# Attention value product by pairs of query tiles, with the context as the stationary operand

## Chip, cores and metric

One Trainium2 chip, of which the kernel uses one core. The metric is the device time of one execution in microseconds (us); the result of a kernel is the median of its runs.

## The reference

One decoder layer on x of 4 batches x 512 tokens x 256 features, float32, with three residual blocks:

```python
x = x + min_gru(layernorm(x))                 # forward and backward recurrence, then W_out
x = x + cross_attention(layernorm(x), ctx)    # the part that changes
x = x + product_key_ffn(layernorm(x))

# cross attention: ctx is (4, 1601, 256), one head
q = x @ Wq.T; k = ctx @ Wk.T; v = ctx @ Wv.T
out = softmax(q @ k.T / 16) @ v
```

The kernel folds the weights: M = Wq.T Wk is made once, the scores are (x M) ctx.T, and the values are (P ctx) Wv.T, so that only the context itself is an operand of the two large products. P is the matrix of exponentials, which is not normalised; its row sums divide the result.

## The kernel before

The kernel has three stages: `stage_gru`, `stage_attention` and `stage_ffn`. The first two share one block of code for each engine, so that they run into each other; the third begins when all engines are through the second.

Large products are done in split form: an operand is held as a high half (fp32r, copied by ScalarE) and a low half (original minus high, made by VectorE, or by GpSimd for the context), and a product is three matmuls, high x high, high x low, low x high (`split_products`, L75 to L77, and L984 to L986).

**Tiles and slots.** The 2048 tokens are 16 query tiles of 128 rows (`TILES`), four to a batch (`TPB`). The context of a batch has 1601 rows: 13 tiles of 128 (`CT`, the last one has 65 rows), in four groups (`GROUPS`: 4, 4, 4, 1). The work is a pipeline of slots g = 0 to 17. Slot g begins on TensorE with the scores of tile g: four blocks (`KB`) of up to 402 columns, six matmuls each, into the four banks of pS (`scores`, L950). The items of the slot follow, in the order that `ORDER` (L574) and `at_tile` write out; every engine goes through the same list and does its own part of each item, in order:

- E: exponentials of tile g on ScalarE, two instructions (L800, L803), once VectorE has the row maximum (`row_max`, L859, one reduction per score block).
- P0 to P3 of tile g-1: TensorE transposes the probabilities of one group into a bank of pR (L1018); ScalarE copies it as the high half (`high`, L754), VectorE makes the low half (`low`, L842).
- A0 to A3 of tile g-1: the value product of one group, 3 matmuls of 256 columns per context tile, into pA. The weights are the transposed probabilities, the moving operand is the context (L984 to L986).
- V of tile g-2: ScalarE has copied pA to `val`, multiplied by the inverse row sum (`values`, L761); TensorE transposes it (two transposes, L1023), ScalarE and VectorE make the halves.
- O of tile g-2: the product with Wv, six matmuls of 256 columns; VectorE adds it to x (`output`, L849). S: the moments of the new rows (`new_moments`, L854).
- X and Q: the transposes of the normalised rows of the next batch (two items of four transposes) and their product with M (two items of six matmuls of 512 columns). The rows are normalised by VectorE (`normalise`, L827) at the end of its slot. Slots 16 and 17 hold the X of the next stage.
- F: the first products of the next stage, in slot 17.

V0 and P0 are issued on TensorE ahead of the last score block (`EARLY`, L597), and their low halves on VectorE there too (`LOWS`).

**Banks and waits.** X, Q, P, V and O use the three banks of pR in turn (`RING` = 3, `place` is an item's number in the ring): TensorE takes a bank when the item three places earlier has been read by VectorE. The two transposed halves of P are one buffer each, pTh and pTl.

**Context.** While a batch is worked on, the context of the next comes in: 15 pieces (`PIECES`), eight of the transposed form for the scores and seven of the plain form for the values (six of 128x512, the last 65x256). A slot has four of them, the fourth slot of a batch three (`pieces_at`, L654). SyncE loads a piece into one of four raw buffers, ScalarE copies the high half (`piece_high`, L769), GpSimd makes the low half (L750). ScalarE takes a piece right after P0, P2 and P3 (`BESIDE`, L596, used in L810), and what is left at the end of its list. The scores of the first tile of a batch wait for all 15 pieces:

```python
            if b >= 1 and t == 0:
                pe.wait_ge(piece_lo, PIECES * b)
```

The weights of the next stage (wqh, wql, two pieces in slots 12 and 13, and `down`) have buffers of their own. `roots` and `new_roots` on GpSimd raise variances to the power -1/2.

Of the kernel before, what the change touches and what calls it, by code (L numbers as in the profile page):

```python
# [554 lines left out]
def stage_attention(nc, keep, d, ctx, sems):  # L555
# [18 lines left out]
    ORDER = "V P0 P1 E O P2 S A0 P3 A1 A2 A3"  # L574

    def at_tile(g):
        out = []
        for kind in ORDER.split():
            a = g - {"V": 2, "O": 2, "S": 2, "E": 0}.get(kind[0], 1)
# [3 lines left out]
        ahead = 1 if b == 1 else 0  # L583
        if b < BATCH and g % TPB == 1 - ahead:
            out += [("X", b, 0), ("X", b, 1)]
        if b < BATCH and g % TPB == 2 - ahead:
            out += [("Q", b, 0), ("Q", b, 1)]
        if g == TILES:
            out.insert(out.index(("P", TILES - 1, 3)), ("X", BATCH, 0))
            out.insert(out.index(("A", TILES - 1, 1)), ("X", BATCH, 1))  # L590
        if g == TILES + 1:
            v, o, s = out
            out = [("F", 0, 0), v, ("F", 0, 1), ("X", BATCH + 1, 0), o, ("X", BATCH + 1, 1), s, ("F", 0, 2), ("F", 0, 3)]
        return out

    BESIDE = ("P0", "P2", "P3")  # L596
    EARLY = {"V0": 3, "P0": 3}  # L597

    def between_scores(g, j):

        return [it for it in SLOTS[g] if g < TILES and EARLY.get(f"{it[0]}{it[2]}") == j]

    LOWS = {"V0": 3, "P0": 3}

    def lows(g, j):

        return [it for it in SLOTS[g] if g < TILES and LOWS.get(f"{it[0]}{it[2]}") == j]

# [3 lines left out]
    SLOTS = [at_tile(g) for g in range(TILES + 2)]  # L612
    ring = [it for slot in SLOTS for it in slot if it[0] not in "ESAF"]
# [8 lines left out]
    qT1 = [st.sb(n, [P, DC, SEQ], F32R) for n in ("qT1h", "qT1l")]  # L622
    qT = (qT0, qT1)
    pT = [st.sb(n, [P, CT, P], F32R) for n in ("pTh", "pTl")]
    vT = [st.sb(n, [P, 2, DC, P], F32R) for n in ("vTh", "vTl")]
    val = st.sb("val", [P, 2, D])
# [5 lines left out]
    rinv = st.sb("rinv", [P, 2])  # L632
    stats = st.sb("stats", [P, TILES, 6])
    ve, rstd, ve3 = (st.sb(n, [P, TILES]) for n in ("ve", "rstd", "ve3"))
    halves(st, keep, 1)
# [11 lines left out]
    value_mm, val_ready, x3_ready = st.sem("value_mm"), st.sem("val_ready"), st.sem("x3_ready")  # L647
# [20 lines left out]
    def wait_context(eng, i):  # L668
# [3 lines left out]
        b, n = i // PIECES + 1, i % PIECES  # L672
        if 2 <= b < BATCH:
            if n < DC * -(-CTX // SEQ):
                eng.wait_ge(score_mm, KB * TPB * (b - 1))
            else:
                eng.wait_ge(value_mm, NG * TPB * (b - 1))

    def half(it, which, n):
# [7 lines left out]
        if kind == "P":  # L687
            rows = CLAST if GROUPS[i][-1] == CT - 1 else P
            m = len(GROUPS[i])
            return pT[which][0:rows, GROUPS[i][0]:GROUPS[i][0] + m], \  # L690
                bank[0:rows, 0:m * P].rearrange("p (t n) -> p t n", n=P)
        return vT[which][:, a % 2], bank[:, 0:DC * P].rearrange("p (t n) -> p t n", n=P)

    def wait_overwrite(eng, it):
# [8 lines left out]
        elif kind == "P" and a >= 1:  # L703
            eng.wait_ge(value_mm, NG * (a - 1) + i + 1)
        elif kind == "V" and a >= 2:
            eng.wait_ge(bank_full, place[("O", a - 2, 0)] + 1)

    def sync(sp):
# [5 lines left out]
        sp.dma_start(bq[:], d["fbq"]).then_inc(ld_bq, 16)  # L714
        sp.dma_start(keep["down"][:], d["downT"].rearrange("(k p) n -> p k n", p=P)).then_inc(ld_key, 16)
# [9 lines left out]
    def gpsimd(pool):  # L725
# [15 lines left out]
        for g in range(TILES):  # L741
            if g == 2:
                roots(1, 2 * TPB, TILES)
            if g >= TPB and g % TPB == 2:
                new_roots(g // TPB - 1)
            for i in pieces_at(g):
# [3 lines left out]
                pool.tensor_tensor(lo, raw(i % RAW), hi.bitcast(F32), ALU.subtract).then_inc(piece_lo, 1)  # L750

    def scalar(act):
# [8 lines left out]
        def values(g):  # L761
            act.wait_ge(value_mm, NG * (g + 1))
            act.wait_ge(rinv_ready, g + 1)
            if g >= 2:
                act.wait_ge(bank_full, place[("V", g - 2, 0)] + 1)
            act.activation(val[:, g % 2], pA[:, 0:D], ACT.Copy, scale=rinv[:, g % 2:g % 2 + 1])\
                .then_inc(val_ready, 1)
# [21 lines left out]
        for g in range(TILES + 2):  # L789
            if 0 <= g - 2 < TILES:  # L790
                values(g - 2)
            left = list(pieces_at(g)) if g < TILES else []
            for it in SLOTS[g]:
# [14 lines left out]
                elif it[0] not in "SAO":  # L808
# [6 lines left out]
    def vector(dve):  # L815
# [43 lines left out]
        def row_max(g):  # L859

            h = g % 2
            for j in range(KB):
                for it in lows(g, j):
                    low(it)
# [4 lines left out]
            for it in lows(g, KB):  # L869
                low(it)  # L870
# [22 lines left out]
        for g in range(TILES + 2):  # L893
            if 0 <= g - 1 < TILES:
                h = (g - 1) % 2
                dve.wait_ge(exp_ready, 2 * g)
                if g >= 3:
                    dve.wait_ge(val_ready, g - 2)
                link(dve.tensor_tensor(rowsum[:, h:h + 1], part[:, h, 0:1], part[:, h, 1:2], ALU.add))
                dve.reciprocal(rinv[:, (g - 1) % 2:(g - 1) % 2 + 1], rowsum[:, (g - 1) % 2:(g - 1) % 2 + 1])\  # L900
# [7 lines left out]
            for it in SLOTS[g]:  # L908
                if it[0] == "O":
# [3 lines left out]
                elif it[0] not in "AEF" and it not in [i for j in range(KB + 1) for i in lows(g, j)]:  # L913
                    low(it)
# [5 lines left out]
            if TPB < g < TILES and g % TPB == 1:  # L920
                a = g - 1 - TPB
# [3 lines left out]
            if g >= TILES - 1 and g <= TILES:  # L925
                normalise(BATCH + g - TILES + 1)

    def tensor(pe):
# [42 lines left out]
        def item(it):  # L971
            kind, a, i = it
            if kind == "A":
                pe.wait_ge(bank_free, place[("P", a, i)] + 1)
                if i == 0 and a >= 1:
                    pe.wait_ge(val_ready, a)
                if i == 0 and a == 0:
                    pe.wait_ge(gru["x2_ready"], 2 * BATCH)
                    pe.wait_ge(gru["piece_lo"], PIECES)
                for kt in GROUPS[i]:  # L980
                    rows, par = (CLAST if kt == CT - 1 else P), (a // TPB) % 2
                    l = [p[0:rows, kt] for p in pT]
                    r = [c[par][0:rows, kt] for c in (cNh, cNl)]
                    pe.matmul(pA[:, 0:D], l[0], r[0], start=(kt == 0), stop=False)  # L984
                    pe.matmul(pA[:, 0:D], l[0], r[1], start=False, stop=False)  # L985
                    last = pe.matmul(pA[:, 0:D], l[1], r[0], start=False, stop=(kt == CT - 1))  # L986
# [33 lines left out]
            elif kind == "V":  # L1020
                pe.wait_ge(val_ready, a + 1)
                for k in range(DC):
                    last = pe.transpose(bank[:, k * P:(k + 1) * P], val[:, a % 2, k * P:(k + 1) * P], ident[:])  # L1023
            else:
                pe.wait_ge(bank_free, place[("V", a, 0)] + 1)
                last = split_products(pe, bank[:, 0:D], [
                    ((vT[0][:, a % 2, k], vT[1][:, a % 2, k]), (WvTh[:, k], WvTl[:, k])) for k in range(DC)])
            last.then_inc(bank_full, 1)

        for g in range(TILES + 2):  # L1030
# [5 lines left out]
            for it in SLOTS[g]:  # L1036
                if it[0] not in "ES" and it not in early(g):
# [5 lines left out]
def stage_ffn(nc, keep, d):  # L1043
# [28 lines left out]
    with ExitStack() as ctx:  # L1072
        st = Stage(nc, ctx, "ffn")
        down = keep["down"]
# [772 lines left out]
def program(nc, d):  # L1847
    with ExitStack() as ctx:
# [5 lines left out]
        for n in ("wqh", "wql"):  # L1854
            keep[n] = st.sb(n, [P, DC, QC * P], F32R)
# [78 lines left out]
```

## Time and profile before

| | us |
|---|---|
| median of 3 runs | 416.8 |
| lowest and highest | 416.44, 419.18 |
| the profiled execution, its own time | 418.28 |
| its span, first to last instruction | 416.4 |

The profile is of one execution. Its rows give, for an engine (PE is TensorE, PEld its weight loads, DVE VectorE, ACT ScalarE, POOL GpSimd), the start and duration of instructions, and what ended the idle time before them. Matmuls overlap: the time that one costs is the distance between two starts, not its duration. Instructions of one kind in a row are merged (x4), and the time is then that of all.

### The profile page before, as it was taken

Reading aid. Unit: us, or ns where it says so; the run is one execution under the profiler, and the core shown is the slowest. Engines: PE = TensorE matmul, PEld = TensorE weight load, DVE = VectorE, ACT = ScalarE, POOL = GpSimd, SP = SyncE. Lnnn points to the kernel's source line nnn. Section 1 sums busy time; section 2 is a strip of 40 time slices with the busy share of each in tenths; the row PEclk is TensorE's granted clock in tenths of the full one; section 3 lists DMA queues with packets and bytes.
Section 4 is the critical chain, followed back from the end, with each engine's and each line's share of the span. In section 5 each row is a group of like instructions: output and inputs, shape, how many; then the busy total and the mean of one; then the engine's idle time right before and its main releaser. Section 6 shows DMA issues by size and latency. Waiting matters only on the chain. (4 is left out here: it accounts for less than half of the span.)

```text
span 416.4 us, 7868 instructions
## 1 busy us (share of the span) xinstructions
PE 396.5 (95%) x2569; PEld 366.5 (88%) x2569; DVE 296.9 (71%) x1104; ACT 243.7 (59%) x535; POOL 215.9 (52%) x208
## 2 busy tenths in 40 slices
PE   1999999999999999999999999999999979999877
PEld 1788888899899999999999999999778979999766
DVE  4889677786466676457575555565785998899996
ACT  3687759354465655456574534444566878677362
POOL 2588999764253224334333212000147777889994
PEclk9999999999999999999999999999999987999999
DMA  7800223004422222221232100000100000000101
GB/s 229 291 0 3 76 56 100 9 5 126 108 67 64 55 80 76 60 78 53 58 96 58 54 2 2 0 2 0 28 1 2 0 3 1 27 26 28 41 25 65
DMA packets 19992, 21.38 MB, mean 51 GB/s; under 512 B 3180, under 2 KB 16624, under 8 KB 19952
## 3 DMA queue, kind: packets, MB, share of 16 engines
q1 hardware_dynamic: 18832, 19.96, 16.4%
q10 hardware_dynamic: 1120, 0.92, 0.7%
q8 instruction: 21, 0.34, 0.4%
q14 instruction: 19, 0.16, 0.1%
HBM read 18.78 MB, written 2.10 MB: 50 GB/s over the span
## 5 line engine op out<-in xcount | busy, mean ns | idle before, releaser
L847 DVE TENSOR_TENSOR att_pTl<-context_pR,att_pTh 128x512 fp32r<-128x512 f32 x64 | 37.4, 586 | 26.4 <-ACT att_pTh L759 26.2
L1191 POOL TENSOR_TENSOR ffn_prod<-ffn_first,ffn_near 128x1024 f32<-128x1024 f32 (+1 forms) x29 | 54.1, 1884 | 2.1 <-DVE ffn_first L1591 2.1
L866 DVE TENSOR_REDUCE att_mx<-keep_pQ 128x1 f32<-128x402 f32 x64 | 35.3, 567 | 24.2 <-PE keep_pQ L77 24.2
L759 ACT ACTIVATE att_pTh<-context_pR 128x512 fp32r<-128x512 f32 x64 | 32.4, 516 | 9.8 <-PE context_pR L1018 9.0
L1743 PE MATMUL ffn_pT<-keep_ident,ffn_prod 128*128 128x128 f32 x240 | 31.9, 291 | 6.2 <-POOL ffn_prod L1191 3.7
L1743 PEld LDWEIGHTS ffn_pT<-keep_ident,ffn_prod 128*128 128x128 f32 x240 | 30.0, 153 | 8.6 <-DVE ffn_hT L1622 4.8
L223 POOL TENSOR_TENSOR gru_z<-gru_z,gru_g 128x512 f32<-128x512 f32 x16 | 28.8, 1799 | 7.9 <-DVE gru_g L428 7.9
L1018 PE MATMUL context_pR<-keep_ident,att_prob 128*128 128x128 f32 (+1 forms) x208 | 32.8, 272 | 0.0
L984 PE MATMUL context_pA<-context_cNh,att_pTh 128*128 128x256 f32 (+1 forms) x104 | 31.4, 302 | 0.9 <-DVE att_pTl L847 0.9
L984 PE MATMUL context_pA<-att_cNh,att_pTh 128*128 128x256 f32 (+1 forms) x104 | 31.1, 299 | 0.0
L1553 DVE MAX8 ffn_top<-ffn_e 128x8 f32<-128x32 f32 x256 | 29.2, 177 | 0.4 <-ACT ffn_e L1359 0.2
L750 POOL TENSOR_TENSOR att_cNl<-keep_raw,att_cNh 128x512 fp32r<-128x512 f32 (+1 forms) x14 | 16.7, 1210 | 24.3 <-ACT att_cNh L773 24.3
L985 PE MATMUL context_pA<-context_cNl,att_pTh 128*128 128x256 f32 (+1 forms) x104 | 29.2, 281 | 0.0
L759 ACT ACTIVATE att_vTh<-context_pR 128x256 fp32r<-128x256 f32 x16 | 6.1, 384 | 39.4 <-PE context_pR L1023 39.4
L986 PE MATMUL context_pA<-context_cNh,att_pTl 128*128 128x256 f32 (+1 forms) x104 | 29.1, 280 | 0.0
L986 PE MATMUL context_pA<-att_cNh,att_pTl 128*128 128x256 f32 (+1 forms) x104 | 29.0, 279 | 0.0
L985 PE MATMUL context_pA<-att_cNl,att_pTh 128*128 128x256 f32 (+1 forms) x104 | 29.0, 279 | 0.0
L750 POOL TENSOR_TENSOR att_cTl<-keep_raw,att_cTh 128x512 fp32r<-128x512 f32 (+1 forms) x16 | 15.4, 978 | 25.9 <-ACT att_cTh L773 25.9
L75 PE MATMUL keep_pQ<-gru_xTh,gru_wh 128*128 128x512 f32 x62 | 26.9, 434 | 0.0
L1018 PEld LDWEIGHTS context_pR<-keep_ident,att_prob 128*128 128x128 f32 (+1 forms) x208 | 24.8, 140 | 0.7
L76 PE MATMUL keep_pQ<-gru_xTl,gru_wh 128*128 128x512 f32 x62 | 24.6, 397 | 0.0
L77 PE MATMUL keep_pQ<-gru_xTh,gru_wl 128*128 128x512 f32 x62 | 24.6, 396 | 0.0
(326 smaller groups left out, 1297.3 us busy)
## 6 DMA issues: line engine op xcount, KB each, us to landing
keep_raw<-in_ctxT SPq DMA_DIRECT2D x24, 256.0 KB, 2.6
keep_raw<-in_ctx SPq DMA_DIRECT2D x24, 256.0 KB, 2.8
out<-keep_x SPq DMA_DIRECT2D x16, 128.0 KB, 1.7
keep_x<-in_x SPq DMA_DIRECT2D x3, 512.0 KB, 9.9
gru_wout<-in_W_out SPq DMA_DIRECT2D x1, 512.0 KB, 8.0
keep_raw<-in_fWq SPq DMA_DIRECT2D x2, 256.0 KB
keep_raw<-in_ctxT SPq DMA_DIRECT2D x8, 32.5 KB, 4.1
keep_raw<-in_ctx SPq DMA_DIRECT2D x4, 65.0 KB
```

The costliest lines, as they stand in the source:

```text
L223: pool.tensor_tensor(z[:, n % ZB], z[:, n % ZB], g[:, u % 2], ALU.mult).then_inc(zg_ready, 1)
L750: pool.tensor_tensor(lo, raw(i % RAW), hi.bitcast(F32), ALU.subtract).then_inc(piece_lo, 1)
L759: act.activation(to, bank, ACT.Copy).then_inc(bank_high, 1)
L847: dve.tensor_tensor(to, bank, half(it, 0, n)[0].bitcast(F32), ALU.subtract).then_inc(bank_free, 1)
L866: last = dve.tensor_reduce(mx[:, h, j:j + 1], pS[:, j, 0:min(SPANS[j][1], CTX) - SPANS[j][0]], AX.X, ALU.max)
L984: pe.matmul(pA[:, 0:D], l[0], r[0], start=(kt == 0), stop=False)
L985: pe.matmul(pA[:, 0:D], l[0], r[1], start=False, stop=False)
L986: last = pe.matmul(pA[:, 0:D], l[1], r[0], start=False, stop=(kt == CT - 1))
L1018: last = pe.transpose(bank[0:rows, m * P:(m + 1) * P], prob[:, a % 2, kt * P:kt * P + rows], ident[:])
L1191: return eng.tensor_tensor(prod[:, i % PB, a:b].rearrange("p h (i j) -> p h i j", j=KEYS), (factor if factor is not None else first[:, n % ...
L1553: ins = dve.max(top[:, n % 2, t, h, a:a + 2 * TOPK], e[:, n % 2, t, h, half * KEYS:(half + 1) * KEYS])
L1743: last = pe.matmul(pW[:, i % 2, c * P:(c + 1) * P], prod[:, i % PB, h, c * P:(c + 1) * P], ident[:], start=(h == 0), stop=(c == 0 and h == ...
```

## The change

- Tiles go in pairs (even, odd). pTh and pTl are twice as wide, one half per tile. The value product (items A and B) has the context tile as weights, half of the features each (A the first, B the second), and the transposed probabilities of both tiles as the moving operand, 256 columns. Its result is the transposed value directly, in pA.
- There is no V transpose and no `val`. V is now one copy of pA (512 columns) on ScalarE and one low half on VectorE, per pair.
- The inverse row sum is no longer applied to the values: `output` multiplies by it as it adds to x.
- The order is written out for even and odd slots, with one slot more at the end (g = 18), and own lists for slots 1, 16, 17 and 18. In even slots both O are issued ahead of the third score block and P0, P1 ahead of the fourth.
- ScalarE takes pieces of the context only at the end of its list (`BESIDE` is gone). Which slot has which pieces, and the wait of the scores for them, stay.
- wqh, wql and `down` share the space of the first context buffers; the loads wait for the scores of the third batch. `new_roots` and the variances before it come two slots later.

```diff
-    ORDER = "V P0 P1 E O P2 S A0 P3 A1 A2 A3"
+    EVEN = "O-4 O-3 P0-1 P1-1 P2-1 E S-4 S-3 A0-2 P3-1 A1-2 A2-2 A3-2"
+    ODD = "B0-3 E P0-1 B1-3 P1-1 B2-3 P2-1 B3-3 V-3 P3-1"
...
+        if g == 0:
+            out += [("X", 1, 0), ("X", 1, 1)]
+        if g == 1:
+            out = [("E", 1, 0), ("P", 0, 0), ("P", 0, 1), ("Q", 1, 0), ("P", 0, 2), ("Q", 1, 1), ("P", 0, 3)]
+        if 2 <= b < BATCH and g % TPB == 1:
             out += [("X", b, 0), ("X", b, 1)]
+        if 2 <= b < BATCH and g % TPB == 2:
             out += [("Q", b, 0), ("Q", b, 1)]
         if g == TILES:
+            out = [("X", BATCH, 0), ("O", g - 4, 0), ("P", g - 1, 0), ("X", BATCH, 1), ("O", g - 3, 0), ("P", g - 1, 1),
+                   ("S", g - 4, 0), ("S", g - 3, 0), ("P", g - 1, 2), ("A", g - 2, 0), ("P", g - 1, 3), ("A", g - 2, 1),
+                   ("A", g - 2, 2), ("A", g - 2, 3)]
         if g == TILES + 1:
+            out = [("B", g - 3, 0), ("B", g - 3, 1), ("X", BATCH + 1, 0), ("B", g - 3, 2), ("X", BATCH + 1, 1),
+                   ("B", g - 3, 3), ("V", g - 3, 0), ("F", 0, 0), ("F", 0, 1)]
+        if g == TILES + 2:
+            out = [("O", g - 4, 0), ("O", g - 3, 0), ("S", g - 4, 0), ("S", g - 3, 0), ("F", 0, 2), ("F", 0, 3)]
...
-    BESIDE = ("P0", "P2", "P3")
-    EARLY = {"V0": 3, "P0": 3}
+    EARLY = {"O": (2, 2), "P": (3, 2)}
...
+        if b == BATCH:
+            eng.wait_ge(score_mm, KB * TPB * (BATCH - 1))
...
+        elif kind == "P" and a >= 2:
+            eng.wait_ge(value_mm, NG * (a // 2 * 2 - 1) + i + 1)
...
+        def values_high(p):
+            act.wait_ge(value_mm, 2 * NG * (p + 1))
+            if p >= 1:
+                act.wait_ge(bank_full, place[("O", 2 * p - 1, 0)] + 1)
+            act.activation(vT[0][:].rearrange("p c n -> p (c n)"), pA[:], ACT.Copy).then_inc(value_high, 1)
...
+                elif it[0] == "V":
+                    values_high(it[1] // 2)
+                elif it[0] in "XQP":
                     high(it)
-                if left and f"{it[0]}{it[2]}" in BESIDE:
-                    piece_high(left.pop(0))
             for i in left:
                 piece_high(i)
...
-            dve.tensor_tensor(x_all[:, g], pR[:, n % RING, 0:D], x_all[:, g], ALU.add).then_inc(bank_free, 1)
+            dve.scalar_tensor_tensor(out=x_all[:, g], in0=pR[:, n % RING, 0:D], scalar=rinv[:, g % TPB:g % TPB + 1],
+                                     in1=x_all[:, g], op0=ALU.mult, op1=ALU.add).then_inc(bank_free, 1)
...
+                p, ch = a // 2, "AB".index(kind)
+                if kind == "A":
+                    pe.wait_ge(bank_free, place[("P", a + 1, i)] + 1)
+                    if i == 0 and p >= 1:
+                        pe.wait_ge(value_low, p)
...
+                    out = pA[:, ch * 2 * P:(ch + 1) * 2 * P]
+                    l = [c[par][0:rows, kt, ch * P:(ch + 1) * P] for c in (cNh, cNl)]
+                    r = [t[0:rows, kt] for t in pT]
+                    pe.matmul(out, l[0], r[0], start=(kt == 0), stop=False)
+                    pe.matmul(out, l[0], r[1], start=False, stop=False)
+                    last = pe.matmul(out, l[1], r[0], start=False, stop=(kt == CT - 1))
```

## Rows read from the trace of the kernel before

**Rows 1.** The page, part 1: busy time, share of the span, instructions.
```profile
PE 396.5 (95%) x2569; PEld 366.5 (88%) x2569; DVE 296.9 (71%) x1104; ACT 243.7 (59%) x535; POOL 215.9 (52%) x208
```

**Rows 2.** Busy time by stretch; the last columns: PE clock, DMA share, GB/s.
```profile
95.00:280.00 185.00, 184.15 (x1321) 179.47 (x1319) 112.37 (x274) 96.42 (x207) 55.65 (x53) 1.00 0.20 56
280.00:297.00 17.00, 15.87 (x110) 14.14 (x110) 9.04 (x24) 7.17 (x15) 0.00 (x0) 1.00 0.01 1
```

**Rows 3.** Waits of PE from 95 to 297 us: total, times, longest.
```profile
PE context_pA L984 <- DVE att_pTl L847: 0.9, 2, 0.6
PE context_pR L1023 <- ACT att_val L766: 0.7, 1, 0.7
PE context_pR L75 <- DVE att_vTl L847: 0.2, 1, 0.2
```

**Rows 4.** Timeline from 132 to 136 us, end of slot 3: start, duration, engine.
```profile
132.52 0.69 DVE L847 TENSOR_TENSOR att_pTl<-context_pR,att_pTh 128x512 fp32r<-128x512 f32 x1 [1.49 <-ACT att_pTh L759]
...
133.15 0.28 PE L986 MATMUL context_pA<-context_cNh,att_pTl 128*128 128x256 f32 x1
...
133.27 0.39 PE L984 MATMUL context_pA<-context_cNh,att_pTh 128*128 128x256 f32 x1
...
135.03 0.28 PE L986 MATMUL context_pA<-context_cNh,att_pTl 65*128 65x256 f32 x1
...
135.17 0.42 PE L75 MATMUL keep_pQ<-att_cTh,att_qT1h 128*128 128x402 f32 x1
...
135.34 0.47 ACT L766 ACTIVATE att_val<-context_pA,att_rinv 128x256 f32<-128x256 f32 x1 [1.88 <-PE context_pA L986]
```

**Rows 5.** Timeline of PE, transposes and what follows them, slot 5.
```profile
149.96 0.38 PE L1023 MATMUL context_pR<-keep_ident,att_val 128*128 128x128 f32 x2
150.18 0.60 PE L1018 MATMUL context_pR<-keep_ident,att_prob 128*128 128x128 f32 x4
...
153.19 0.36 PE L984 MATMUL context_pA<-att_cNh,att_pTh 128*128 128x256 f32 x1
153.39 0.28 PE L985 MATMUL context_pA<-att_cNl,att_pTh 128*128 128x256 f32 x1
```

**Rows 6.** Timeline of ACT, end of slot 3.
```profile
131.89 0.60 ACT L759 ACTIVATE att_pTh<-context_pR 128x512 fp32r<-128x512 f32 x1
132.37 0.64 ACT L773 ACTIVATE att_cNh<-keep_raw 128x512 fp32r<-128x512 f32 x1
132.89 0.27 ACT L759 ACTIVATE att_pTh<-context_pR 65x128 fp32r<-65x128 f32 x1
133.05 0.42 ACT L773 ACTIVATE att_cNh<-keep_raw 65x256 fp32r<-65x256 f32 x1
```

**Rows 7.** Timeline of POOL, low halves of the context, slots 2 and 3.
```profile
121.65 3.79 POOL L750 TENSOR_TENSOR att_cNl<-keep_raw,att_cNh 128x512 fp32r<-128x512 f32 x3 [3.32 <-ACT att_cNh L773]
...
133.09 1.98 POOL L750 TENSOR_TENSOR att_cNl<-keep_raw,att_cNh 128x512 fp32r<-128x512 f32 x2 [2.75 <-ACT att_cNh L773]
```

**Rows 8.** Timelines of PE, DVE and ACT in slot 1.
```profile
97.40 0.43 PE L75 MATMUL keep_pQ<-context_cTh,keep_qT0h 128*128 128x402 f32 x1
...
100.80 0.60 PE L1018 MATMUL context_pR<-keep_ident,att_prob 128*128 128x128 f32 x4
...
103.45 0.15 DVE L873 TENSOR_SCALAR att_nmax<-att_tmax 128x1 f32<-128x1 f32 x1
...
103.80 1.26 ACT L800 ACTIVATE att_prob<-keep_pQ,att_nmax 128x1206 f32<-128x1206 f32 x1
...
105.60 0.61 ACT L759 ACTIVATE att_pTh<-context_pR 128x512 fp32r<-128x512 f32 x1
```

**Rows 9.** Timeline of DVE, end of slot 15.
```profile
278.62 1.37 DVE L838 TENSOR_SCALAR att_xn<-keep_x,keep_mv,keep_rstd 128x256 f32<-128x256 f32 x4
```

**Rows 10.** Timeline of PE in the next stage, the same transposes twice.
```profile
343.07 3.49 PE L1743 MATMUL ffn_pT<-keep_ident,ffn_prod 128*128 128x128 f32 x16 [2.48 <-ACT ffn_gT L1313]
...
355.33 1.91 PE L1743 MATMUL ffn_pT<-keep_ident,ffn_prod 128*128 128x128 f32 x16
```

More of the change, by code:

```diff
@@ L610, in early @@
         return [it for j in range(KB) for it in between_scores(g, j)]
-    SLOTS = [at_tile(g) for g in range(TILES + 2)]
-    ring = [it for slot in SLOTS for it in slot if it[0] not in "ESAF"]
+    SLOTS = [at_tile(g) for g in range(TILES + 3)]
+    ring = [it for slot in SLOTS for it in slot if it[0] in "XQPO"]
     place = {it: n for n, it in enumerate(ring)}
@@ L621, in stage_attention @@
     prob = st.sb("prob", [P, 2, CTX])
[L622 to L626, printed above, removed]
     mx = st.sb("mx", [P, 2, KB])
@@ L788, in scalar @@
         last.then_inc(xn_ready, 1)
-        for g in range(TILES + 2):
-            if 0 <= g - 2 < TILES:
-                values(g - 2)
+        for g in range(TILES + 3):
             left = list(pieces_at(g)) if g < TILES else []
@@ L862, in row_max @@
             for j in range(KB):
-                for it in lows(g, j):
-                    low(it)
+                for it in between_scores(g, j):
+                    if it[0] == "O":
+                        output(it[1])
+                    else:
+                        low(it)
                 dve.wait_ge(score_mm, KB * g + j + 1)
@@ L891, in last_residual @@
                 .then_inc(gru["x2_ready"], 1)
-        for g in range(TILES + 2):
+        for g in range(TILES + 3):
             if 0 <= g - 1 < TILES:
@@ L908, in vector @@
             for it in SLOTS[g]:
+                if it in early(g):
+                    continue
                 if it[0] == "O":
@@ L912, in vector @@
                     new_moments(it[1])
-                elif it[0] not in "AEF" and it not in [i for j in range(KB + 1) for i in lows(g, j)]:
+                elif it[0] == "V":
+                    values_low(it[1] // 2)
+                elif it[0] in "XQP":
                     low(it)
@@ L1019, in item @@
                                         ident[:])
[L1020 to L1023, printed above, removed]
-            else:
-                pe.wait_ge(bank_free, place[("V", a, 0)] + 1)
+            else:
+                pe.wait_ge(value_low, a // 2 + 1)
+                cols = slice(a % 2 * P, (a % 2 + 1) * P)
                 last = split_products(pe, bank[:, 0:D], [
-                    ((vT[0][:, a % 2, k], vT[1][:, a % 2, k]), (WvTh[:, k], WvTl[:, k])) for k in range(DC)])
+                    ((vT[0][:, k, cols], vT[1][:, k, cols]), (WvTh[:, k], WvTl[:, k])) for k in range(DC)])
             last.then_inc(bank_full, 1)
-        for g in range(TILES + 2):
+        for g in range(TILES + 3):
             if g < TILES:
@@ L1036, in tensor @@
             for it in SLOTS[g]:
-                if it[0] not in "ES" and it not in early(g):
+                if it[0] not in "ESV" and it not in early(g):
                     item(it)
@@ L1073, in stage_ffn @@
         st = Stage(nc, ctx, "ffn")
+        for n in ("wqh", "wql"):
+            st.sb(n, [P, DC, QC * P], F32R)
+        st.sb("down", [P, DC, D])
         down = keep["down"]
@@ L1865, in program @@
         keep["pQ"] = st.ps("pQ", [P, 4, SEQ])
+        with ExitStack() as late:
+            over = Stage(nc, late, "over")
+            for n in ("wqh", "wql"):
+                keep[n] = over.sb(n, [P, DC, QC * P], F32R)
+            keep["down"] = over.sb("down", [P, DC, D])
         with ExitStack() as inner, ExitStack() as sems:
```

86 lines of the change are left out of this document (32 added, 54 removed).

## Prediction

> **What bounds the kernel now.** I read the shares of the page first: TensorE (PE) is busy 95% of the span, every other engine 71% or less [rows 1]. Then the stretches: from 95 to 280 us, where the sixteen attention slots run, PE is busy 184.15 of 185.00 us at full clock, while VectorE (DVE), ScalarE (ACT) and GpSimd (POOL) have 39 to 70% of their time free; the tail of the attention, 280 to 297, is much the same [rows 2]. Last its waits: in 95 to 297 us PE waited 0.9 us for the low halves of the probabilities and 0.7 us for the values, 1.8 us with one small wait more [rows 3]. So time comes off here only by taking work out of PE's in-order stream, and whatever lets PE wait is paid in full. 185 us over sixteen slots is about 11.5 us a slot.
>
> **The value product itself.** Before, 13 context tiles x 3 products of 256 columns per query tile; after, for a pair, 2 channel halves x 13 x 3, again of 256 columns (two tiles wide): 39 per tile either way, 0.12 us from start to start (133.15 to 133.27 in [rows 4]). Operands change sides, the shapes don't. The nearest rows bound such a product by 0.12 below and by 0.20, that of the first one after a transpose [rows 5], above; I take 0.12, the row of the same shape with its weights loaded ahead, and no change.
>
> **What is removed.**
> - Two transposes of values per tile: 149.96 to 150.18, 0.22 us [rows 5]; x16 = 3.5 us.
> - The first product after a transpose takes 0.20 instead of 0.12 us [rows 5]. Now there are four such places in a slot (score block 3, O, A0, A1). After, an even slot has three (block 3, A0, A1) and an odd slot four (B1, B2, B3, next score), so one less in each of 8 pairs: 0.6 us.
> - A2 waits at a hair for the low half of P2: that ends at 132.52 + 0.69 = 133.21, A2's first product starts at 133.27 and lasts 0.39 instead of the 0.28 of the one before [rows 4]. In the even slots after, P2 is copied ahead of the exponential and the low half is there over a microsecond early; in the odd slots the B groups read finished halves. 12 slots (3 to 14) x 0.10 = 1.2 us.
> - The three waits of [rows 3], 1.8 us: P0 and P1 now come a whole group ahead, and the values go through ACT and DVE beside other PE work.
> Together 7.1 us. ACT and DVE lose passes too (one copy of 256 columns on ACT per tile), which is worth nothing: they don't bound. The row scale in the residual addition turns a DVE addition of 256 columns into one with a scalar: bounds 0 and 0.4 us each, taken 0; DVE has the room [rows 2]. On SP the load of the down weights and six key loads now stand behind the scores of tile 11; their first reader is in the next stage, more than four slots (46 us) later, which covers them: 0. Behind them on that queue stands nothing but the end of the attention. The roots of the third normalisation move by two slots on POOL and are read at the tail: 0.
>
> **What is added: the end of a batch.** Slots 3, 7 and 11 must finish the context of the next batch, and scores of slots 4, 8 and 12 wait for all 15 pieces on PE. Before, the last three pieces of a batch (two of 128x512, one of 65x256) are copied on ACT beside P0, P2 and P3 in mid slot. Even so POOL's last low half ends at 133.09 + 1.98 = 135.07 [rows 7] and PE starts at 135.17 [rows 4]: there is no slack. After, ACT takes pieces only at the end of its list, and in an odd slot that list ends with V (which waits for B3) and P3. Let t be the start of B3's last product; PE could go on at t + 0.15.
> - ACT takes a finished pA 0.31 after that (135.03 to 135.34 [rows 4]); it is still 0.08 late from P2. V, 512 columns, 0.48 (131.89 to 132.37 [rows 6]); P3, 0.16 (132.89 to 133.05). First piece copy at t + 1.04.
> - POOL starts its low half 0.72 after a copy starts (132.37 to 133.09 [rows 6, 7]): t + 1.76. Two full ones at 3.79 / 3 = 1.26 and a short one at 1.98 - 1.26 = 0.72 [rows 7]: 3.24, so t + 5.00. PE follows 0.10 later (135.07 to 135.17).
> PE waits 5.1 - 0.15, about 4.9 us, x3 = 14.7 us. Behind the waiting product on PE stands everything; nothing is ready to be moved past it. Bounds: 2.5 us each if POOL were already one piece ahead, 6 if DVE's low halves slow POOL.
>
> **What is added: the first pair.** Slot 1 now has only P and Q work after its scores. ACT does E(1) before it frees the banks of P0. Three score blocks take 97.40 to 100.80, the fourth 1.1 more, so they end at 101.9. The maximum, now out at 103.45 + 0.15 with the low half of P0 (0.6) ahead of it, is ready at 103.0; E takes 103.80 to 105.60 = 1.80 [rows 8], so P0's copy ends at 105.3, its low half at 106.0. PE has P0.0 and P0.1 (0.7) and Q0 (12 x 0.12 = 1.5, for six of 512 columns) to do, is at P0.2, whose bank is P0.0's (ring of three), at 104.1 and goes on at 106.1; Q1 waits a little more. About 2.2 us (bounds 0 and 3).
>
> **What is added: slot 16.** It now begins with X, the transpose of the rows that DVE normalises at the end of slot 15; that stands behind V's low half (t + 0.95 to 1.56), P3's (to 1.8) and takes 1.37 [rows 9]: t + 3.15, and PE waits 3.1 us. Before, X came after seven other items. X, O, P, X, O, P, P then go through three banks; each needs 1.1 to 1.4 us of ACT and DVE per reuse against 1.1 us of PE work: 0.7 us. The X at the end of slots 5 and 9 delays the next P by 0.2 us each, 0.4 together. The rest of the tail has the products of F as cover for V.
>
> Sum: -7.1 + 14.7 + 2.2 + 3.8 + 0.4 = +14.0 us.
>
> **The clock.** PE's clock stands at full speed through the attention [rows 2]. Around 343 us, after an idle stretch of 2.48 us that followed light work, 16 transposes took 3.49 us, and the same ones at 355 us took 1.91 [rows 10]: the half clock (1.2 against 2.4 GHz) cost 1.6 us. Waits of 4.9 us in a dense stream are longer than that one, but come after dense work. Bounds 0 and 2 x 1.6 for each of the three; I take one such loss for two of three, 3.2 us.
> The Trainium skill, TensorE: Matmul & The Clock Gate, section on HAM oscillation, speaks against the change here: the clock is dropped in each long gap and must be earned back after each. By it every batch boundary starts at 1.2 GHz; the trace has no gap of this length after dense work to show it. It would be the rival "clock" below.
>
> Against the profiled execution (span 416.4, 418.28 us in all) this gives 418.28 + 17.2 = 435.5 us; that execution is 1.5 above the median of the runs, 416.8, so the forecast for the median is **434.0 us**, with an own range of 428 to 440.
>
> **The rivals.**
> - Boundary waits half hidden: POOL finds one piece done and waits for less than two low halves, 2.5 us x 3, and the clock stays up. For it: POOL has 70% of the stretch free [rows 2]. Against: all three copies stand behind V in the same list. 416.8 - 7.1 + 7.5 + 6.4 = 423.6.
> - The other side: the boundary costs nothing, because the three pieces reach POOL before B3 ends. Its place is ACT's order in slots 3, 7 and 11, its price is the 14.7 us and the clock's 3.2; it decides as soon as the first copy starts 5 us ahead of the slot's end. For it: ACT is free 48% of the stretch. Against: ACT's order is fixed and V waits for B3. 434.0 - 17.9 = 416.1, no change.
> - Nor do slots 1 and 16 wait: PE's own stream then decides alone, 416.8 - 7.1 = 409.7.
> - Clock: it falls at each wait, for two such losses at each boundary and one each in slots 1 and 16: 8 x 1.6 = 12.8 instead of 3.2, 443.6.
> - The change doesn't do what it says: products with the context as weights stream at another pace. 624 products x 0.01 us are 6 us either way; the same shapes speak against it, and it is in the own range.
>
> **How the numbers follow.** Forecast 0.68, half hidden 0.10, clock 0.08, no boundary 0.08, no waits at all 0.06. Slower by over 1% (4.2 us, about what a measurement of this kernel can tell from no change) holds the first three, 0.86; within 1% 0.08; faster 0.06. The range of 423 to 442 holds the forecast, most of the half-hidden case and the edge of the clock case.
>
> **What would show it.** PE waits of some 5 us on POOL's low halves of the context ahead of the first scores of tiles 4, 8 and 12; one of 2 us in slot 1 and one of 3 us at X of slot 16; a pair of slots without a wait some 0.7 us shorter than now; no line for the transposes of values; 624 value products as before; the stage after the attention as long as before. The prediction is wrong if POOL's low halves end before the slot does, if a pair without waits is no shorter than now, or if the clock falls in more than the three places.

## The result, and the profile after

The changed kernel takes 438.52 us (median of 7 runs, 437.40 to 441.99). The kernel before took 416.47 us in 7 runs on the same chip. The ratio is 1.0517, with an interval of 1.0491 to 1.0543: the change costs 22 us. The profiled execution of the changed kernel took 441.99 us, with a span of 440.2 us. Against the profile of before (418.28 and 416.4 us) that is 23.8 us more, and the ledger below adds up to this pair.

First the shares. From the page of the kernel after, engine, busy time, share of the span and number of instructions:

```profile
PE 401.5 (91%) x2537; PEld 372.1 (85%) x2537; DVE 304.0 (69%) x1096; ACT 234.8 (53%) x511; POOL 216.8 (49%) x208
```

PE's share is down from the 95% of [rows 1]: the kernel now waits. The same two stretches as in [rows 2], of the kernel after (length, busy time and instructions of PE, PEld, DVE, ACT and POOL, granted clock of PE, DMA share, GB/s):

```profile
95.00:280.00 185.00, 167.95 (x1141) 163.43 (x1140) 109.68 (x238) 82.48 (x173) 54.15 (x52) 0.94 0.20 56
280.00:297.00 17.00, 13.81 (x105) 13.59 (x104) 8.52 (x25) 5.69 (x14) 1.67 (x1) 0.96 0.00 1
```

PE idles 17 of 185 us where it idled less than 1, and its granted clock is 0.94 instead of 1.00. Both are new. All of the loss lies in the attention: the first product of the next stage starts at 296.85 us before and at 320.57 us after, 23.7 us later, which is the whole difference. The waits of PE in 84 to 330 us of the kernel after (what is started, what it waited for, us in total, times, longest):

```profile
PE keep_pQ L75 <- issue: 14.1, 3, 4.7
...
PE context_pR L1023 <- DVE att_xn L838: 3.2, 1, 3.2
...
PE context_pR L1033 <- DVE att_pTl L847: 2.0, 1, 2.0
...
PE context_pR L1023 <- DVE att_pTl L847: 1.0, 2, 0.5
```

Four lines for the four costs of the prediction: three waits of the scores at a batch boundary, X in slot 16, P0.2 in slot 1, and X in slots 5 and 9, which waits for a bank that holds a P (the prediction had the P behind X wait). Together 20.3 us, where [rows 3] had 1.8.

**One boundary.** The timeline of PE in the kernel after, at the end of slot 3 (start, duration, engine, line, operation, idle time before it and its releaser). The first row is P3.3 of slot 3, the others the first score block of slot 4:

```profile
130.72 0.27 PE L1033 MATMUL context_pR<-keep_ident,att_prob 128*65 128x128 f32 x1
135.70 0.67 PE L75 MATMUL keep_pQ<-att_cTh,att_qT1h 128*128 128x402 f32 x1 [4.70 <-issue]
```

The same stretch on ACT and then POOL, as [rows 6, 7] had it for before:

```profile
130.57 0.60 ACT L762 ACTIVATE att_pTh<-context_pR 128x512 fp32r<-128x512 f32 x1 [1.25 <-PE context_pR L1033]
131.06 0.59 ACT L769 ACTIVATE att_vTh<-context_pA 128x512 fp32r<-128x512 f32 x1
131.54 0.27 ACT L762 ACTIVATE att_pTh<-context_pR 65x128 fp32r<-65x128 f32 x1
131.70 1.45 ACT L775 ACTIVATE att_cNh<-keep_raw 128x512 fp32r<-128x512 f32 x3
```

```profile
132.40 3.19 POOL L752 TENSOR_TENSOR att_cNl<-keep_raw,att_cNh 128x512 fp32r<-128x512 f32 x3 [7.84 <-ACT att_cNh L775]
```

P2, V, P3 and only then the three pieces (two full, the short one among the x3); POOL had idled 7.84 us before the first. It ends at 132.40 + 3.19 = 135.59, and PE starts 0.11 us later. "issue" as the releaser of a wait of 4.7 us says only that the view named nobody; POOL's end shows who it was.

**Slot 16.** DVE in the kernel after, ahead of X:

```profile
294.30 0.68 DVE L861 TENSOR_TENSOR att_vTl<-context_pA,att_vTh 128x512 fp32r<-128x512 f32 x1
294.90 0.28 DVE L847 TENSOR_TENSOR att_pTl<-context_pR,att_pTh 65x128 fp32r<-65x128 f32 x1
295.16 1.37 DVE L838 TENSOR_SCALAR att_xn<-keep_x,keep_mv,keep_rstd 128x256 f32<-128x256 f32 x4
```

and what waits for it on PE:

```profile
296.68 1.08 PE L1023 MATMUL context_pR<-keep_ident,att_xn 128*128 128x128 f32 x4 [3.19 <-DVE att_xn L838]
```

**Slot 1.** First ACT's exponential of tile 1, then PE's P0.2 of tile 0 (and the rows merged with it), which waits for a bank whose copy stands behind that exponential:

```profile
103.16 1.27 ACT L800 ACTIVATE att_prob<-keep_pQ,att_nmax 128x1206 f32<-128x1206 f32 x1 [3.03 <-DVE att_nmax L883]
```

```profile
106.35 0.66 PE L1033 MATMUL context_pR<-keep_ident,att_prob 128*128 128x128 f32 x4 [1.95 <-DVE att_pTl L847]
```

**The clock.** PE alone, five short stretches of the kernel after (length, PE busy and its instructions, granted clock, DMA share, GB/s):

```profile
107.00:111.50 4.50, 4.50 (x16) 0.62 0.01 4
...
134.70:138.10 3.40, 2.40 (x7) 0.58 0.57 162
...
189.30:196.10 6.80, 5.51 (x19) 0.54 0.30 82
...
243.90:250.80 6.90, 3.83 (x12) 0.54 0.27 82
...
295.10:301.90 6.80, 5.22 (x25) 0.54 0.00 0
```

The clock fell around each of the five long waits, to 1.2 GHz. Work at half clock takes twice its time, so as an estimate half of the busy time in such a stretch is lost: 1.2, 2.75, 1.9 and 2.6 us in the last four, and 4.5 x (1 - 0.62) = 1.7 us in slot 1. That is 10.1 us together, against 3.2 in the forecast. Kernels in which the clock held (e4 below) measure the same losses from start to start: about 6.0 us at the three boundaries and 1.9 in slot 16, so 9.6 us in all, and the ledger uses these.

**A pair without waits.** The first exponential of tiles 13 and 15, two slots apart, on ACT, in the kernel after:

```profile
257.14 1.27 ACT L800 ACTIVATE att_prob<-keep_pQ,att_nmax 128x1206 f32<-128x1206 f32 x1 [0.25 <-DVE att_nmax L883]
...
279.34 1.27 ACT L800 ACTIVATE att_prob<-keep_pQ,att_nmax 128x1206 f32<-128x1206 f32 x1 [0.25 <-DVE att_nmax L883]
```

and in the kernel before:

```profile
251.99 1.27 ACT L800 ACTIVATE att_prob<-keep_pQ,att_nmax 128x1206 f32<-128x1206 f32 x1
...
274.83 1.27 ACT L800 ACTIVATE att_prob<-keep_pQ,att_nmax 128x1206 f32<-128x1206 f32 x1
```

22.20 us for a pair of slots instead of 22.84: the change does shorten the steady part, by 0.64 us a pair, and loses more than that at five places.

### The profile page after: what moved, and what is told of

Its sections match the earlier page's. It is cut to its first block and busy times, and to the rows that moved or that the text cites. A ratio compares the mean times of both kernels' runs of the same rounds, so it can differ in the third digit from the quotient of the medians.

```text
span 440.2 us, 7700 instructions
## 1 busy us (share of the span) xinstructions
PE 401.5 (91%) x2537; PEld 372.1 (85%) x2537; DVE 304.0 (69%) x1096; ACT 234.8 (53%) x511; POOL 216.8 (49%) x208
## 5 line engine op out<-in xcount | busy, mean ns | idle before, releaser
L800 ACT ACTIVATE att_prob<-keep_pQ,att_nmax 128x1206 f32<-128x1206 f32 x16 | 20.3, 1270 | 43.8 <-DVE att_nmax L883 43.8
L1758 PEld LDWEIGHTS ffn_pT<-keep_ident,ffn_prod 128*128 128x128 f32 x240 | 29.0, 149 | 9.0 <-DVE ffn_hT L1637 4.8
L75 PE MATMUL keep_pQ<-att_cTh,att_qT1h 128*128 128x402 f32 (+1 forms) x64 | 24.2, 378 | 9.4 <-issue 9.4
L999 PE MATMUL context_pA<-att_pTh,context_cNh 128*128 128x256 f32 (+1 forms) x104 | 30.8, 296 | 0.0
L999 PE MATMUL context_pA<-att_pTh,att_cNh 128*128 128x256 f32 (+1 forms) x104 | 30.7, 295 | 0.0
L1001 PE MATMUL context_pA<-att_pTh,att_cNl 128*128 128x256 f32 (+1 forms) x104 | 29.1, 280 | 0.0
L1001 PE MATMUL context_pA<-att_pTh,context_cNl 128*128 128x256 f32 (+1 forms) x104 | 29.1, 280 | 0.0
L1000 PE MATMUL context_pA<-att_pTl,att_cNh 128*128 128x256 f32 (+1 forms) x104 | 29.1, 280 | 0.0
L1000 PE MATMUL context_pA<-att_pTl,context_cNh 128*128 128x256 f32 (+1 forms) x104 | 29.0, 279 | 0.0
L75 PE MATMUL keep_pQ<-context_cTh,keep_qT0h 128*128 128x402 f32 (+1 forms) x64 | 24.2, 378 | 4.7 <-issue 4.7
```

The source lines that it names most:

```text
L75: pe.matmul(out, lh, rh, start=(i == 0), stop=False)
L999: pe.matmul(out, l[0], r[0], start=(kt == 0), stop=False)
L1000: pe.matmul(out, l[0], r[1], start=False, stop=False)
L1001: last = pe.matmul(out, l[1], r[0], start=False, stop=(kt == CT - 1))
L1758: last = pe.matmul(pW[:, i % 2, c * P:(c + 1) * P], prod[:, i % PB, h, c * P:(c + 1) * P], ident[:], start=(h == 0), stop=(c == 0 and h == ...
```

## The experiments

The theory: the change gains about 5 us in PE's stream and pays for five waits that come from the order of the lists of ACT and DVE, each with its loss of clock behind it. The rivals: the new product itself (its operand roles, the residual addition with a scalar) is what costs; the waits cost their length alone; or the waits are a matter of POOL's speed and not of the order. Medians are in us; the runs of before that stand beside them have medians of 418.20 (e1 to e4), 416.97 (f1 to f4) and 416.83 (f5), so kernels of different groups are compared by their ratios to before.

| kernel | median | lowest, highest | ratio to before, interval |
|---|---|---|---|
| after | 438.52 | 437.40, 441.99 | 1.0517, 1.0491 to 1.0543 |
| e1_front | 420.14 | 419.38, 421.69 | 1.0054, 1.0030 to 1.0077 |
| e2_beside | 424.04 | 422.33, 424.38 | 1.0140, 1.0106 to 1.0174 |
| e3_scorewait | 419.33 | 416.42, 420.64 | 1.0038, 1.0011 to 1.0064 |
| e4_filler | 433.26 | 432.68, 434.12 | 1.0371, 1.0339 to 1.0402 |
| f1_slot1 | 416.23 | 414.54, 417.62 | 0.9974, 0.9952 to 0.9995 |
| f2_slot16 | 413.88 | 412.99, 416.67 | 0.9942, 0.9913 to 0.9971 |
| f3_both | 411.65 | 410.71, 413.12 | 0.9876, 0.9851 to 0.9902 |
| f4_transposes | 414.92 | 414.09, 416.25 | 0.9948, 0.9928 to 0.9967 |
| f5_before_late | 421.60 | 421.36, 421.70 | 1.0105, 1.0071 to 1.0138 |

### The boundary: three ways to take the wait away

**e1_front.** ACT copies the pieces at the head of its list in the last slot of a batch:

```diff
+            if g % TPB == TPB - 1:
+                for i in left:
+                    piece_high(i)
+                left = []
             for it in items:
```

> The changed kernel (438.5 us), but in slots 3, 7 and 11 ACT copies its three context pieces at the head of its list instead of the end. Theory order: the three waits of 4.7 us (14.1) go, and with them the half clock after each (about 1.2 + 2.75 + 1.9 = 5.9 us, read from the stretches at half clock): 418.5 us, 417 to 420. Rival structure: the waits are where the loss shows, but the value product by pairs is itself slower or something else is late next; then PE waits elsewhere and the time stays above 430.

Measured: 420.14 us, 18.4 below the kernel after (19.3 by the ratios). The boundary waits are gone, and POOL's work is the same, so it was the order and not POOL's speed. What came in their place, PE's waits on the probabilities in 84 to 330 us:

```profile
PE context_pR L1037 <- DVE att_pTl L851: 3.1, 3, 1.9
```

One is the 1.95 us of slot 1; two of 0.6 us, at P3 of slots 7 and 11, are new. Now ACT waits at the head of its list for the load of a piece, and the exponentials and P stand behind it:

```profile
ACT att_cNh L775 <- DMA keep_raw<-in_ctx: 6.7, 4, 2.5
```

**e2_beside.** A piece right after each of P0, P1 and P2 in those slots:

```diff
                     high(it)
+                    if left and g % TPB == TPB - 1 and it[0] == "P":
+                        piece_high(left.pop(0))
```

> The changed kernel, but in slots 3, 7 and 11 ACT takes one piece right after each of P0, P1 and P2, the way it was before. Theory order: the first copy then starts at the P0 copy, some 3.4 us earlier, and POOL's last low half ends about 1.7 us after PE is ready instead of 4.7: 3 x 3.0 = 9 us less wait, and 429.5 if the clock still falls as it did, 423.6 if it stays up. Rival, that the batch boundary is cheap in itself: no change, 438.

Measured: 424.04 us. The wait at the boundary is shorter but there, because P2 comes late in an odd slot:

```profile
PE keep_pQ L75 <- DVE att_pTl L849: 4.1, 3, 1.4
```

The releaser that the view names is not the last one: POOL's third low half ends at 131.78 us (128.55 + 3.23) and PE starts at 131.89, 0.11 later, as in the kernel after. Behind these waits of up to 1.4 us the granted clock stayed at 1.00.

**e3_scorewait.** ACT's list as in the change; instead the scores wait only for the eight pieces of the transposed form, which are what they read, and the value product waits for all 15:

```diff
-                pe.wait_ge(piece_lo, PIECES * b)
+                pe.wait_ge(piece_lo, PIECES * (b - 1) + DC * -(-CTX // SEQ))
...
+                    if i == 0 and a >= TPB and a % TPB == 0:
+                        pe.wait_ge(piece_lo, PIECES * (a // TPB))
```

> The changed kernel with ACT's order as it is, but the scores of tiles 4, 8 and 12 wait only for the eight pieces that they read, and the first value product of a batch, two slots later, waits for all 15. Theory order: as good as the copies at the head, 418.5 us, because POOL's last low halves are wanted only two slots later; PE's waits at the boundaries are gone. Rival (the late copies themselves cost, by keeping ACT and POOL busy into the next slot): between 420 and 430.

Measured: 419.33 us, 19.2 below the kernel after (20.0 by the ratios), the lowest of the three though not clear of e1, with no wait at a boundary and none new. That answers to 14.1 us of waits and 5.85 us of clock (1.2 + 2.75 + 1.9), which make 19.95. The value product as the change has it is in all three kernels, and they come within 1.4% of before: the product isn't what costs the 22 us.

### The clock by itself

**e4_filler.** The boundary waits stay, but PE is busy in them with 38 products whose results are overwritten:

```diff
             if b >= 1 and t == 0:
+                pe.wait_ge(exp_ready, 2 * g - 1)
+                for _ in range(38):
+                    pe.matmul(pS[:, 0, 0:D], Mh[:, 0, 0:P], Mh[:, 1], start=True, stop=True)
```

> The changed kernel with 38 products of 256 columns into a free score bank (results unused) ahead of each of the three boundary waits, some 4.5 us of dense work in place of 4.7 us idle. The wait itself stays paid. If the half clock after a wait is a cost of its own: the clock stays at full speed at the boundaries and the time falls by 5.9 us to about 432.6, 431 to 434. If the clock doesn't matter (ACT or DVE would have held PE back anyway): 438.5. If the clock falls for another reason: no change either.

Measured: 433.26 us, 5.3 below the kernel after; by the two ratios 1.46% or 6.1 us, with some 1.8 us of uncertainty. PE's timeline at the first boundary:

```profile
130.21 4.79 PE L969 MATMUL keep_pQ<-keep_Mh 128*128 128x256 f32 x38
...
135.14 0.45 PE L75 MATMUL keep_pQ<-att_cTh,att_qT1h 128*128 128x402 f32 x1
```

The first score product starts 4.96 us after the last instruction of slot 3 (130.18 to 135.14), as late as in the kernel after, where these are 4.98 us (130.72 to 135.70). It lasts 0.45 us here and 0.67 there. From it to the first exponential of the same tile are 8.23 us here (135.14 to 143.37) and 9.57 in the kernel after (135.70 to 145.27); at the second and third boundary 8.27 and 8.24 against 10.97 and 10.17. The differences, 1.3, 2.7 and 1.9 us, are the price of the clock at the three boundaries, some 6.0 us. So a wait cost its length and the clock behind it. The whole times hold one thing more: in the profiled execution of e4 the clock also held behind the wait of 3.19 us at X of slot 16, which this edit doesn't touch. X to the first product of the next stage takes 22.00 us in it (290.10 to 312.10) and 23.89 in the kernel after (296.68 to 320.57), so there the clock cost 1.9 us.

### Slots 1 and 16

Both on e3, one place each.

**f1_slot1.** P0.0 and P0.1 stand ahead of the exponential of tile 1:

```diff
-            out = [("E", 1, 0), ("P", 0, 0), ("P", 0, 1), ("Q", 1, 0), ("P", 0, 2), ("Q", 1, 1), ("P", 0, 3)]
+            out = [("P", 0, 0), ("P", 0, 1), ("E", 1, 0), ("Q", 1, 0), ("P", 0, 2), ("Q", 1, 1), ("P", 0, 3)]
```

> e3_scorewait (419.3 us) with ACT copying P0.0 and P0.1 of tile 0 ahead of the exponential of tile 1 instead of behind it. Theory: PE's wait at P0.2 (1.95 us) goes, a new one of about 0.6 us shows at P0.3, behind the copy of Q; and the 3.4 us at half clock that follow the wait now (1.7 us lost) go: 416.2 us. If the clock falls anyway: 417.9. If slot 1 has slack behind it: no change.

Measured: ratio 0.9974 against e3's 1.0038, 0.64% or 2.7 us, give or take 1.4 (3.1 us by the medians). The wait of 1.95 us is one of 0.5 us, and the half clock behind it is gone: 1.45 + 1.7 = 3.15 by the rows. In the profiled execution the clock held in slot 16 too, behind a wait that the edit leaves as it was; so one profile of each doesn't show that an edit alone kept the clock up.

**f2_slot16.** The rows for X are normalised a slot earlier, and P stands ahead of O:

```diff
-            out = [("X", BATCH, 0), ("O", g - 4, 0), ("P", g - 1, 0), ("X", BATCH, 1), ("O", g - 3, 0), ("P", g - 1, 1),
+            out = [("X", BATCH, 0), ("P", g - 1, 0), ("O", g - 4, 0), ("X", BATCH, 1), ("O", g - 3, 0), ("P", g - 1, 1),
...
-            if TILES - 1 <= g <= TILES:
-                normalise(BATCH + g - TILES + 1)
+            if g in (TILES - 2, TILES):
+                normalise(BATCH + (g == TILES))
```

> e3_scorewait with the rows for X of slot 16 normalised at the end of slot 14 instead of 15, and P0 ahead of O in slot 16. Theory: PE no longer waits 3.2 us at X but about 0.8 us at O, for the low half of V, and the 3.4 us at half clock after it go too: -2.4 and -1.7, less 0.6 us for the banks, 415.8 us. If the clock falls anyway: 417.5.

Measured: 0.9942, 0.96% or 4.0 us less than e3, give or take 1.6 (5.45 by the medians). X no longer waits; a P waits 0.5 us in its place, not O 0.8, and in slot 16 the clock holds. By the rows that is 2.7 us of wait and 0.9 us of clock (X to the next stage's first product takes 22.9 us in e3 and 22.0 in f1, where the clock held), and not the 1.7 us of clock that I had expected.

**f3_both.** f1 and f2 together.

> e3_scorewait with both edits, f1 and f2: 419.3 - 3.1 - 3.5 = 412.7 us if they add up, 410 to 414. It is then faster than the kernel before by about 1%, which is the 7.1 us of removed work and waits less some 2 us that are left in slots 1, 5, 9 and 16. Rival (the removed PE work of 3.5 us was not on the path): 416 or more.

Measured: 411.65 us, ratio 0.9876 (0.9851 to 0.9902): 1.2% faster than the kernel before, and the fastest of all. The first stretch of [rows 2] in this kernel:

```profile
95.00:280.00 185.00, 182.73 (x1320) 178.36 (x1319) 123.48 (x278) 91.21 (x192) 55.40 (x53) 1.00 0.19 56
```

The granted clock is 1.00 again, and all that PE still waits for in 84 to 330 us, small change aside, is:

```profile
PE context_pR L1025 <- DVE att_pTl L847: 1.0, 2, 0.5
PE context_pR L1035 <- DVE att_qT1l L847: 0.5, 1, 0.5
PE context_pR L1035 <- DVE att_pTl L847: 0.5, 1, 0.5
```

### What the removed transposes were worth

**f4_transposes.** f3 with two transposes of the identity into the bank of each O, which the product then overwrites: the same number and place per tile as the removed ones, with nothing to wait for.

```diff
+                for k in range(DC):
+                    pe.transpose(bank[:, k * P:(k + 1) * P], ident[:], ident[:])
```

> f3_both with two transposes of the identity into the bank of each O, overwritten by it: the removed transposes of values put back as pure PE work, results unused. Theory (PE's stream sets the time): 16 x (0.22 + 0.08 for the first product after a transpose) = 4.8 us more than f3_both. Rival (something beside PE sets the pace of a slot): less than 2 us.

Measured: 414.92 us, 3.3 above f3 (0.72% or 3.0 us by the ratios, give or take 1.3). I had expected 4.8, with a slower product after each group of transposes in it. The time rules out 4.8 only just; that the slower product costs nothing is read from the rows. PE's timeline at one O:

```profile
128.80 0.38 PE L1040 MATMUL context_pR<-keep_ident 128*128 128x128 f32 x2
128.93 0.36 PE L75 MATMUL context_pR<-keep_WvTh,att_vTh 128*128 128x256 f32 x1
129.14 0.28 PE L76 MATMUL context_pR<-keep_WvTl,att_vTh 128*128 128x256 f32 x1
```

From the first transpose to the second product are 0.34 us. Two transposes and one product of 0.12 account for all of it: 0.22 + 0.12. The 0.20 us from the first product to the second, which I had read in [rows 5] as a price of the switch, is the transposes' own time showing up late.

### The rule of the boundary on the old kernel

**f5_before_late.** The kernel before, with its pieces at the end of ACT's list:

```diff
-    BESIDE = ("P0", "P2", "P3")
+    BESIDE = ()
```

> The kernel before with one edit: ACT takes the context pieces only at the end of its list (the list of pieces beside P0, P2 and P3 is empty). The same edit in the old order: P3's copy ends at 133.05, POOL starts 0.72 later and works 3.24, so PE waits from 135.17 to about 137.1, 1.9 us at each of three boundaries: 5.8 us more than before if the clock stays up, 10 more if each wait costs one stretch at half clock too. Rival (the late pieces matter only in the new order): no change.

Measured: 421.60 us, ratio 1.0105: 4.4 us lost (2.9 to 5.8), with nothing of the pairs in it. PE's waits, and POOL at the first boundary:

```profile
PE keep_pQ L75 <- issue: 3.8, 3, 1.3
```

```profile
133.13 3.21 POOL L750 TENSOR_TENSOR att_cNl<-keep_raw,att_cNh 128x512 fp32r<-128x512 f32 x3 [6.42 <-ACT att_cNh L773]
```

POOL's chain is the same, 3.2 us for three pieces. The wait is 1.3 us here (1.9 expected) and 4.7 in the kernel after. A slot of before ends with value products behind P3, which cover most of the chain; an odd slot of the pairs ends with P3 and V, which stand ahead of the pieces on ACT and leave no cover on PE. In the old order the edit of `BESIDE` costs 4.4 us; the boundaries cost 20 only with the new order as well.

## Why the prediction was right, and where it was off

Forecast 434.0, measured 438.5, inside the range of 423 to 442 and the forecast's own 428 to 440; the sign and the five places were right. One of its own signs of being wrong came true all the same: "if the clock falls in more than the three places". By its steps, with the profiled pair:

| step | forecast, us | measured, us | from |
|---|---|---|---|
| two transposes of values, x16 | -3.5 | -3.3 | f4 |
| first product after a transpose | -0.6 | 0 | f4's timeline |
| A2 at a hair | -1.2 | -1.2 | what is left of a pair, (0.64 - 0.44), over the same six pairs |
| waits of [rows 3] | -1.8 | -1.8 | none of these left |
| three boundaries | +14.7 | +14.1 | 4.70, 4.67, 4.71 |
| slot 1 | +2.2 | +1.95 | timeline |
| slot 16: X, then the ring | +3.1, +0.7 | +3.2, 0 | timeline, waits; ring 0.5 in e4 |
| X in slots 5 and 9 | +0.4 | +1.0 | waits |
| clock | +3.2 | +9.6 | 1.7 in slot 1 by the windows; 6.0 and 1.9 against e4 |
| sum | +17.2 | +23.6 | the next stage's first product is 23.7 late |

- **The waits.** The chain from B3 over ACT's list to POOL was right link by link: three pieces on POOL in 3.19 us (3.24 forecast), PE 0.11 behind them, the wait 4.7 instead of 4.9. Slot 1 and X of slot 16 came within 0.3 us. The ring of slot 16 shows in no row of the kernel after, where PE runs that stretch at half clock. It is there where the clock held, in e4 (and as much in f1), at the second X and the P behind it:

```profile
292.15 0.66 PE L1026 MATMUL context_pR<-keep_ident,att_xn 128*128 128x128 f32 x4 [0.27 <-DVE keep_xT0l L847]
...
294.22 0.66 PE L1036 MATMUL context_pR<-keep_ident,att_prob 128*128 128x128 f32 x4 [0.26 <-DVE keep_xT0l L847]
```

That is 0.5 us for the 0.7 forecast; in the kernel after the slower PE hides it. At X in slots 5 and 9 I had 0.2 us for what is 0.5. All waits together were forecast at 21.1 us and are 20.3.
- **The gains.** The pair without waits is 0.64 us shorter; forecast were 0.7 (0.44 for the transposes, 0.2 for A2, 0.07 for the switch). Without the switch the sum is 0.64, as measured; the 0.2 of A2 is a remainder that no run took by itself. The gains were forecast 0.8 us too large and the waits 0.8 us too large, and these two misses cancel. A count of gaps between starts must not take the late part of one operation for a price of the next.
- **The failed step** is the clock: "I take one such loss for two of three, 3.2 us". The clock fell at all three boundaries and behind the shorter waits of slots 1 and 16 too, and a loss was 1.3 to 2.7 us and not always 1.6. That is five losses for two, 9.6 us for 3.2, and the mis-sized term is all of the distance in the profiled pair: 435.5 + 6.4 = 441.9 against 441.99. That execution is the slowest of the seven and has the lowest mean granted clock, 0.961; the others have 0.965 to 0.969. So at the median the term is smaller, by some 1.8 us as an estimate, (0.965 - 0.961) x 440; that the forecast is only 4.5 us off the median is in part luck.
- **Where the price came from.** The "clock" rival was nearer (12.8 us at the same five places), and I gave it 0.08 because [rows 10] had their idle stretch after light work. I had read those rows wrongly. The trace of before has two stretches at half clock in the next stage, and the wait of 2.48 us set off neither. Windows of PE around both, and the work of the second (the clock is the last figure but two):

```profile
338.00:340.00 2.00, 2.00 (x17) 0.85 0.00 0
...
350.00:353.00 3.00, 3.00 (x16) 0.50 0.00 0
```

```profile
348.01 2.05 PE L1713 MATMUL ffn_pK<-ffn_group_of,ffn_sq 128*128 128x4 f32 x16 [0.44 <-ACT ffn_sq L1343]
349.92 3.47 PE L1743 MATMUL ffn_pT<-keep_ident,ffn_prod 128*128 128x128 f32 x16
```

The first time the clock had fallen before 340.0, while PE was busy and before the wait began; the second time 16 transposes took 3.47 us again with no longer wait ahead of them than 0.44 us. Both falls came in or behind products of 4 columns (128x4 in the row). So the trace held no price for a wait after dense work, and 1.6 us per wait was an assumption. The Trainium skill, TensorE: Matmul & The Clock Gate, section on HAM oscillation, named the danger of long gaps; the traces agree at the three waits of 4.7 us. The falls at 3.19 and 1.95 us are this case's own.
- **The other rivals.** "Half hidden" fell with POOL's 7.84 us of idle time before the first piece: it was not one piece ahead. "The boundary costs nothing" is what e3 is, by another edit; "no waits at all" gave 409.7, and f3, which is nearly that kernel, takes 411.65 with 2 us of waits left. The operand roles made no difference: value products start 0.117 us apart in either kernel, and f3 would otherwise not beat before. The addition with a scalar takes 0.48 us instead of 0.42 and is hidden on DVE.

## What to carry to other kernels

When an order is rewritten, ask for each item that feeds the next block what now stands ahead of it on every in-order queue of its chain; here three small copies at the end of ACT's list cost more than all that the new product saved, and asking for only the operand that a product reads (e3) gave it back without moving a copy. A wait on TensorE in a dense stretch can cost more than its length: price the clock loss behind it too (1.3 to 2.7 us in the kernel after, from a wait of 1.95 us on) before arguing that it might be spared. An algebraic gain of a few tenths per slot shows only as such waits go: e3 was no faster than before, f1 and f2 were by 0.3 and 0.6%, f3 by 1.2%.

## What the runs showed of the hardware

**The clock can fall around short waits in dense work.** In the kernel after it fell at waits of 1.95, 3.19 and 4.7 us; in e2 and f5 it held after waits of 1.4 and 1.3 us. Length alone doesn't decide. Slot 16 has the same wait of 3.2 us in e3, e4 and f1, and the clock fell in e3 and held in e4 and f1; PE's windows around it in e3, X starting at 274.83 (the clock is the last figure but two):

```profile
273.13:274.83 1.70, 0.00 (x0) 1.00 0.00 0
274.83:276.53 1.70, 1.70 (x14) 0.90 0.00 0
276.53:278.23 1.70, 1.69 (x9) 0.50 0.00 0
278.23:279.93 1.70, 1.70 (x11) 0.59 0.00 0
```

and in f1, X starting at 271.93 after 3.20 us:

```profile
270.23:271.93 1.70, 0.01 (x1) 1.00 0.00 0
271.93:273.63 1.70, 1.70 (x14) 1.00 0.00 0
273.63:275.33 1.70, 1.42 (x13) 1.00 0.00 0
275.33:277.03 1.70, 1.43 (x14) 1.00 0.00 0
```

In e3 the clock fell only after PE had taken up work again: at 0.90 in the first stretch behind the wait, most of it still ran at full speed. In the kernel after it fell at the boundaries and in slot 16 during the wait; at the third, with PE starting at 246.97:

```profile
244.00:244.40 0.40, 0.00 (x0) 1.00 0.00 0
244.50:245.50 1.00, 0.00 (x0) 0.50 0.00 0
```

The half clock lasted some 3.4 us (slot 1, first boundary) or 6.8 us (second, third and slot 16), and the part of it that lies in the wait costs nothing (some 2.5 us at the third boundary); that is why equal waits cost 1.3 to 2.7 us on top. What makes e4 and f1 escape wasn't tried and stays open. It need not be an edit: executions of one kernel differ too. The seven of the kernel after go from 437.4 us at a mean clock of 0.969 to 441.99 at 0.961, the six of f2 from 412.99 at 0.992 to 416.67 at 0.984; only the profiled one has a trace that shows where.

**A transpose of 128x128 in f32 costs some 0.11 us from start to start**, two of them 0.22 [rows 5], and the rows of f4 show no price for going from transposes to products.
